# Identity attention with E as the stationary operand: weighing straight into the output layout

## The reference, cut to what matters

```python
def _L0_attn_ref(x):                       # x = layernorm(h), (64, 128, 256)
    xh = x.reshape(B, T, H, hd)            # H = 16, hd = 16, T = 128
    x_centered = xh - jnp.mean(xh, axis=1, keepdims=True)
    corr = jnp.einsum('bthd,bThd->bhtT', x_centered, x_centered)
    corr = jax.nn.softmax(corr, axis=-1)
    out = jnp.einsum('bhtT,bThd->bthd', corr, xh)
    return out.reshape(B, T, D)
h = h + _L0_attn_ref(_layernorm(h, axis=-1))
```

## Time and profile before

| | |
|---|---|
| median of the runs | 2725.2 us |
| the profiled execution: its time, its span | 2724.97 us, 2723.2 us |
| mean granted TensorE clock | 0.987 |
| busy in the span: TensorE, its weight loads, VectorE, ScalarE, GpSimd | 2600.6, 2225.9, 1931.3, 1703.1, 1389.7 us |

### The profile page before, as it was taken

One profiled execution on the slowest core, in us unless ns is written; L12 is line 12 of the kernel. 1 busy time (PEld: TensorE's weight loads), 2 busy tenths in 40 slices (PEclk: granted clock), 3 DMA queues, 4 the chain that ended last, 5 costly groups with the idle time before them and its releaser, 6 DMA issues.

```text
span 2723.2 us, 71565 instructions
## 1 busy us (share of the span) xinstructions
PE 2600.6 (95%) x25088; PEld 2225.9 (82%) x25088; DVE 1931.3 (71%) x3771; ACT 1703.1 (63%) x4184; POOL 1389.7 (51%) x1396
## 2 busy tenths in 40 slices
PE   6999999869999999998999998999999998999998
PEld 4888888747888888886888886888888887788887
DVE  5777777658778787876656556877777777666664
ACT  3666666647778777774444444777777777444442
POOL 7888888567666666662000007666666665000000
PEclk9999999979999999999999999999999999999999
DMA  1111111111111111112111111111111111222221
GB/s 43 37 49 36 44 38 35 37 50 47 41 40 38 37 40 40 40 52 75 51 58 49 56 48 49 39 37 40 40 38 37 40 40 54 70 66 80 80 73 47
DMA packets 165609, 130.30 MB, mean 48 GB/s; under 512 B 23239, under 2 KB 163689, under 8 KB 165462
## 3 DMA queue, kind: packets, MB, share of 16 engines
q1 hardware_dynamic: 163157, 119.80, 14.2%
q0 software_dynamic: 2304, 8.47, 1.1%
HBM read 77.47 MB, written 50.33 MB: 47 GB/s over the span
## 4 chain that ended last, share of the span: by engine, by line
PE 30%; DVE 20%; ACT 20%; issue 6%; SPq 2%; DMA 1%; DVEq 0%; ACTq 0%
ACT attn_E L1036 15%; PE const_banks L1313 6%; PE const_banks L1314 6%; PE const_banks L1315 6%; DVE attn_neg_top L1209 6%; DVE attn_ss L1202 5%; DVE attn_rot_b L1186 5%; ACT attn_sq L1073 5%; PE const_banks L1447 3%; PE const_banks L1449 3%; PE const_banks L1448 3%; SPq L899 2%; DVE attn_E L1164 2%; PE const_banks L1297 1%; DVE attn_rsum L1162 1%
## 5 line engine op out<-in xcount | busy, mean ns | idle before, releaser
L1036 ACT ACTIVATE attn_E<-const_banks,attn_nbias,attn_rn 128x128 f32<-128x128 f32 x1024 | 453.2, 462 | 154.6 <-DVE attn_nbias L1214 154.6
L969 POOL TENSOR_TENSOR attn_qk<-attn_rot_a,attn_rot_b 128x1024 f32<-128x1024 f32 x128 | 303.5, 2371 | 421.8 <-issue 324.4
L956 POOL TENSOR_TENSOR ffn_rstd<-ffn_var,const_neg_half 128x4 f32<-128x4 f32 x32 | 32.3, 1011 | 687.9 <-DVE ffn_var L1139 687.9
L1324 PE MATMUL const_banks<-weights_w_hi,attn_xT_hi 128*128 128x512 f32 x768 | 315.9, 411 | 4.9 <-ACT attn_sq L1073 2.5
L1326 PE MATMUL const_banks<-weights_w_hi,attn_xT_lo 128*128 128x512 f32 x768 | 305.0, 397 | 0.0
L1325 PE MATMUL const_banks<-weights_w_lo,attn_xT_hi 128*128 128x512 f32 x768 | 303.2, 395 | 0.0
L1239 DVE SCALAR_TENSOR_TENSOR ffn_gated<-const_banks,weights_b_col,ffn_gate 128x512 f32<-128x512 f32 (+1 forms) x192 | 143.7, 748 | 215.7 <-ACT ffn_gate L1107 208.6
L1313 PE MATMUL const_banks<-ffn_xT_hi,ffn_w_hi 128*128 128x512 f32 x704 | 283.2, 402 | 6.9 <-DVE ffn_xT_lo L1151 5.4
L1314 PE MATMUL const_banks<-ffn_xT_lo,ffn_w_hi 128*128 128x512 f32 x704 | 280.1, 398 | 0.0
L1315 PE MATMUL const_banks<-ffn_xT_hi,ffn_w_lo 128*128 128x512 f32 x704 | 279.8, 398 | 0.0
L1107 ACT ACTIVATE ffn_gate<-const_banks,weights_b_col 128x512 f32<-128x512 f32 x160 | 110.2, 689 | 227.1 <-PE const_banks L1315 221.7
(11 more groups left out here) (178 smaller groups left out, 7967.4 us busy)
## 6 DMA issues: line engine op xcount, KB each, us to landing
attn_x_res<-xa SPq DMA_DIRECT2D x128, 128.0 KB, 4.7
xb<-attn_x_new SPq DMA_DIRECT2D x128, 128.0 KB, 1.7
ffn_x_<-xb SPq DMA_DIRECT2D x32, 512.0 KB
h<-ident_h SPq DMA_DIRECT2D x64, 128.0 KB, 1.7
xa<-ident_n SPq DMA_DIRECT2D x64, 128.0 KB, 1.7
attn_x_<-xa SPq DMA_DIRECT2D x128, 64.0 KB
xa<-ffn_x_new SPq DMA_DIRECT2D x16, 512.0 KB, 3.6
ffn_add<-h SPq DMA_DIRECT2D x16, 512.0 KB, 6.7
```

Source lines behind the costliest of these rows:

```text
L969: pool.tensor_tensor(qk[:, slot].rearrange("p a n -> p (a n)"), rot_a[:].rearrange("p a h d -> p (a h d)"), rot_b[:].rearrange("p a h d -> ...
L1036: last = act.activation(E[:, r, i], ps_s[:, r, i * P:(i + 1) * P], ACT.Exp, bias=nbias[:, r, i:i + 1], scale=rn[:, slot, h:h + 1], accum_o ...
L1324: pe.matmul(out_, xT_hi[:, slot, k], w.w_hi[:, k, cols], start=(k == 0), stop=False)
```

## The change

The weighing swaps its operands: a head's 128 x 128 block of E is the stationary operand, the head's 128 x 32 block of values and ones the moving one. The result has the tokens on the partitions and goes straight to the head's 32 columns of `ps_out`. The transposes (TURN), the tile `outT` and ScalarE's copy disappear; the waits on `outT_ps` become waits on `out_ps`, those on `outT_ready` go or become others (the centring now waits for the copy of the transposed maxima, the weighing for the product of the row before, `att_done`). On VectorE, reciprocal and product stand ahead of the maxima.

```diff
-    OUT, STAT, CENT, SCORE, WEIGH, TURN, DONE, STORE = 8, 9, 10, 11, 12, 13, 13, 14
+    OUT, STAT, CENT, SCORE, WEIGH, DONE, STORE = 8, 9, 10, 11, 12, 13, 14
-        outT = n.sb("outT", [P, 4, P])
 # ScalarE
                         for g in range(2):
                             need(act, s["shifted"], b + 1)
-                            need(act, s["outT_ps"], b - 1)
+                            need(act, s["out_ps"], b - 1)
...
-                    if on(WEIGH):
-                        b = t - WEIGH
-                        need(act, s["outT_ps"], b + 1)
-                        need(act, s["out_ps"], b)
-                        act.activation(outT[:], ps_turn, ACT.Copy).then_inc(s["outT_ready"], 1)
 # VectorE: the block "if on(SCORE)" (maxima) now stands behind "if on(DONE)" (reciprocal, product)
-                        need(dve, s["outT_ps"], b - 3)
+                        need(dve, s["out_ps"], b - 3)
 # TensorE
-                    if on(TURN):
-                        b = t - TURN
-                        need(pe, s["outT_ready"], b + 1)
-                        need(pe, s["att_done"], b)
-                        for j in range(4):
-                            last = pe.transpose(ps_out[:, 4 * j:4 * j + 4].rearrange("p h d -> p (h d)"), outT[:, j],
-                                                c["ident"][:])
-                        last.then_inc(s["out_ps"], 1)
 # the centring
-                        need(pe, s["outT_ready"], b - 2)
+                        need(pe, s["mT_ready"], b - 1)
 # the transpose of the maxima
-                        need(pe, s["outT_ready"], b - 1)
 # the weighing
                         need(pe, s["exp_done"], 2 * b + 2)
-                        need(pe, s["mT_ready"], min_int(t - SCORE + 1, ROWS))
-                        need(pe, s["cT_ready"], min_int(t - CENT + 1, ROWS))
-                        need(pe, s["outT_ready"], b)
-                        for j in range(4):
-                            for k in range(4):
-                                last = pe.matmul(ps_turn[W * k:W * k + W, j], v1[:, slot, 4 * j + k],
-                                                 E[:, slot % 2, k, j * P:(j + 1) * P], start=True, stop=True,
-                                                 skip_group_check=True)
-                        last.then_inc(s["outT_ps"], 1)
+                        need(pe, s["att_done"], b)
+                        for k in range(4):
+                            for j in range(4):
+                                last = pe.matmul(ps_out[:, 4 * j + k], E[:, slot % 2, k, j * P:(j + 1) * P],
+                                                 v1[:, slot, 4 * j + k], start=True, stop=True)
+                        last.then_inc(s["out_ps"], 1)
```

More of the change, by code:

```diff
@@ L187, in front @@
             "stat", "aggr", "eps", "rstd", "norm", "cT_ps", "cT_ready", "S_ps", "max_done", "mT_ps", "mT_ready",
-            "shifted", "exp_done", "outT_ps", "outT_ready", "out_ps", "recip", "att_done", "h2_done", "stat2",
+            "shifted", "exp_done", "out_ps", "recip", "att_done", "h2_done", "stat2",
             "aggr2", "eps2", "rstd2", "prod2", "n2_ready", "n2_done")}
@@ L407, in body @@
                         silu(t - 1, 1)
[L408 to L416, removed]
                     if on(DONE):
@@ L427, in body @@
                                           ).then_inc(s["att_done"], 1)
+                    if on(SCORE):
+                        b = t - SCORE
+                        for g in range(2):
+                            need(dve, s["S_ps"], b + 1)
+                            need(dve, s["mT_ps"], b)
+                            dve.tensor_reduce(top[:, 2 * g:2 * g + 2, 0:4],
+                                              ps_S[:, 2 * g:2 * g + 2].rearrange("p k (j t) -> p k j t", j=4), AX_X,
+                                              ALU.max).then_inc(s["max_done"], 1)
                     if on(STAT):
```

## The result

The changed kernel takes 2963.2 us (2960.8 to 2968.6, four runs) against 2725.1 (2724.4 to 2729.0, four runs): slower by 238 us, ratio 1.087 (95% interval 1.086 to 1.089). I had forecast 2854. The profiled execution takes 2965.68 us.

The account below looks back on a forecast made before the run. TensorE was taken as the bound, idle 0.5 us from 100 to 500 us; 60 turns x 1.95 = 117 plus drain 4 + 8 gave +129 on 2724.97, 2854 us. Range 2805 to 2925.

Parts of the forecast that it names:

- weighing to scores: TensorE's front turn: 31 further passes at 111 ns, 3.44 us, plus 0.20 us until the scores start.
- the slack at the maxima's transpose: TensorE's front turn: the slack before this transpose falls from 0.64 to 0.14 us, without a stall.
- the drain's two weighings: Last two weighings, after row output has ended: 8.4 us at full clock, 15.3 us with both weighings doubled at half clock.
- 60 x 1.95 + 4: 60 front turns each 1.95 us longer (117 us), plus 4 us for three drain turns without row output.
- the 8 us that I had booked there: Last two weighings at the drain's end: +8 us, taking the granted clock as half; the other end was +1.
- the change to quarter tiles: Between hidden matmul and weighing: about 0.2 of 0.43 us, won back by a full-array load; otherwise add 0.2 us.
- the clock's term: TensorE's clock in the front: no added time, since falls follow real idleness and the weighing has no gap.
- the first rival: The clock falls in the front because weighing streams little: 1.7 us every turn, +109, 2963 us; chance 0.16.
- no pace under 48 ns in f32: Rival at the weighing: loads hidden or faster, 34 ns a pass, not slower, at most -29 us, 2696; chance 0.05.
- no pace of 192: Rival at the weighing: loads do not overlap short streams, 192 ns a pass, +2.5 us a turn, 3015 us; chance 0.05.
- no waits that took the added time in: Rival: added time partly falls into unseen waits, or loads run nearer 80 ns; 60 to 80 us slower, 2795; chance 0.05.
- VectorE's order, priced at nothing: VectorE's divide ahead of the maxima: 0.26 + 0.42 us fit under the scores' 1.10 us, so no added time.

Follow-up runs that it names:

- wide128: The changed kernel with each weighing matmul streaming the values of four heads (128 columns) instead of one (32), same 32 weight loads: 2852.8 us.
- after_b_old: The changed kernel with E and a VectorE-made copy of the values in bf16 for the weighing, and VectorE's old order (maxima first): 2731.8 us.

## Why the prediction was wrong

**Right.** The loads of E are 128 columns wide and 192 ns long, and a pass takes 111 ns with 32 streamed columns as with 128; weighing to scores is 3.58 us at full clock (I had 3.64). In wide128, where the clock stays up, the 63 turns from first to last weighing take 611.1 us, 9.70 each where I had 9.65: 2.00 us more than before, not 1.95. Part of the rest is the centring, which now starts behind the scores' small tiles and takes 1.16 us instead of 1.06. TensorE waited for nothing between 100 and 500 us, so the slack at the maxima's transpose held: in wide128's turn of 311.48 the maxima end at 315.08 and their transpose starts at 315.35. In the changed kernel the drain's two weighings took 789.55 - 774.57 = 15.0 us (15.3).

That wide128 measured 2852.8 for my 2854 is partly luck. Up to the last weighing but one it took 125.2 us more than the kernel before, where I had 60 x 1.95 + 4 = 121. Its last two weighings took 8.4 us, as I had worked out for full clock, against 7.45; the 8 us that I had booked there were for half clock. One reading was off too: of the 0.43 us between hidden matmul and weighing I put 0.2 down to the change to quarter tiles, while the row itself names a wait of the weight loads for the exponentials of 0.25 us.

**The step that failed** is the clock's term: the sum has it at zero, on the argument that falls follow real idleness and that the weighing has no gap, which also left the first rival a chance of only 0.16. What happened is that rival: last weighing less first is 720.8 us in the changed kernel and 611.1 in wide128, so 110 us or 1.74 a turn. I had written 1.7 a turn, +109, 2963 in all. The mechanism was the rival's, but that the figure fits so well is luck: I took it from one fall elsewhere and charged it to every turn, while 16 of 52 turns lose nothing, 16 lose 1.6 us and 20 lose 3.1.

The argument itself fails in the runs: TensorE was busy without a gap, its weight loads 3.54 of the 3.58 us of the weighing of 317.48, and the clock fell all the same; giving it more columns to stream, or dense work between, stopped it. Idleness before a fall is one way to it, and the rows before had it: the fall of 1219 stands behind a wait of 3.27 us,

```profile
1218.51 1.23 PE L1369 MATMUL const_banks<-const_ident,attn_qk 128*128 128x128 f32 x8 [3.27 <-POOL attn_qk L980]
```

and I took the one way for the only one. The other quiet stretch of the earlier trace rows had 22 matmuls in 3.2 us, and there idleness and too little streaming could not be told apart.

The Trainium skill ("TensorE: Matmul & The Clock Gate", section "HAM oscillation — how this bites in real kernels") ties the swing of the clock to waits of microseconds between bursts of matmuls. The fall of 1219 agrees with that; the changed kernel has the swing with no wait at all. The Trainium skill (same page, section "Back-to-back issue gap") has matmuls of up to 64 columns follow each other every 25 ns or so; here that holds over bf16 loads, 25 ns, and not over f32 loads, 111. The Trainium skill (same page, section "LDWEIGHTS (loading the stationary operand)") makes a load of 128 columns 107 ns; here f32 loads follow each other every 111 ns and bf16 loads every 25.

**The other rivals** fell: no pace under 48 ns in f32, no pace of 192, no waits that took the added time in. VectorE's order, priced at nothing, was nothing or 9 us in the changed kernel, and 34 us alone on the kernel before (0.0126 x 2725).

## What to carry to other kernels

Swapping the operands so that the large block is stationary trades streamed columns for loaded ones. In f32 a full-width load cost 111 ns a pass here, where four narrow ones had run side by side, and the swap lost time even with half the loads (2740.6); it paid only with bf16 loads, 25 ns, and there by what it took off the chain through the exponentials. And a stretch of 3.6 us in which TensorE mainly loads took its clock down even at 100% busy: spread such passes among dense ones, or let them stream more columns under the same loads, which cost nothing here. Before a reorder on another engine is booked at zero, look at what its first wait is for: the same two blocks cost 34 us in one kernel.

## What the runs showed of the hardware that I had not expected

Adding streamed columns made a kernel faster: 32, 64 and 128 columns under the same 32 loads gave 2963, 2862 and 2853 us. And VectorE's value instruction took 0.41 us where it ran clear of GpSimd's two-operand subtraction (median before), and 1.43 us each of the 34 times from 100 to 500 us in after_b_old that it ran beside one from start to end. Only VectorE's was the longer for it: the subtraction kept to 1.26 to 1.30 us. No run moved the one against the other on purpose, so this is seen in the traces and not tested:

```profile
307.52 0.67 DVE L447 TENSOR_SCALAR ident_vb<-tok_h,ident_mv,ident_rstd 128x256 bf16<-128x256 f32 x1 [0.25 <-POOL ident_rstd L299]
...
308.11 1.43 DVE L450 TENSOR_SCALAR ident_v<-tok_h,ident_mv,ident_rstd 128x256 f32<-128x256 f32 x1
308.12 1.27 POOL L278 TENSOR_TENSOR tok_hid_lo<-tok_hid,tok_hid_hi 128x512 fp32r<-128x512 f32 x1
```
